# An attention step on one Trainium2 core: VectorE's addition of the projected output moves ahead of the log-sigmoid, and one normalisation moves into the next step

## The reference

```python
x = x + 0.5 * ffn(layernorm(x))        # 8 experts, the best 2 of each token
x = x + attn(layernorm(x))
x = x + 0.5 * ffn(layernorm(x))

def attn(x):                            # 16 heads of 8 features
    q, k, v = x @ Wq, x @ Wk, x @ Wv    # split into heads
    c = cumsum(log_sigmoid(x @ Wf))     # per head, along the sequence
    scores = q @ k.T * 8 ** -0.5 + c[:, None] - c[None, :]
    scores = where(causal, scores, -1e30)
    return (softmax(scores) @ v) @ Wo
```

## Time and profile before

| what | us |
|---|---|
| median of 3 runs | 460.31 |
| the three runs | 458.33, 460.38, 460.31 |
| the profiled execution | 458.89 |
| its span, first to last instruction | 456.8 |

### The profile page before, as it was taken

How to read it: one execution, slowest core, us unless ns; L and a number is a source line. 1 busy time by engine, 2 the same in 40 slices (tenths; PEclk the granted TensorE clock), 3 DMA queues, 4 the chain that set the end, 5 groups by cost and what they waited for, 6 DMA issues and landing times.

```text
span 456.8 us, 11688 instructions
## 1 busy us (share of the span) xinstructions
PE 398.6 (87%) x3280; PEld 285.1 (62%) x3296; DVE 363.6 (80%) x1284; ACT 274.9 (60%) x758; POOL 251.7 (55%) x431
## 2 busy tenths in 40 slices
PE   0778888775799999999999999999998989888884
PEld 0656666562566676667667666767776756666652
DVE  3889999987777877786797678778776459999985
ACT  4666777442266575666657566666666666667753
POOL 8977656444155536544554554455445526676654
PEclk9999999888899999999999999999999999999999
DMA  4221000025554454364355435444550000010001
GB/s 114 82 69 22 2 1 0 1 89 161 139 140 137 137 140 135 106 169 113 115 139 138 132 108 166 114 125 135 152 135 10 6 2 0 26 45 25 23 23 46
DMA packets 45024, 39.11 MB, mean 86 GB/s; under 512 B 5128, under 2 KB 41756, under 8 KB 44986
## 3 DMA queue, kind: packets, MB, share of 16 engines
q1 hardware_dynamic: 44986, 38.66, 30.2%
HBM read 22.61 MB, written 15.20 MB: 83 GB/s over the span
## 4 chain that ended last, share of the span: by engine, by line
PE 41%; POOL 24%; issue 18%; DVE 12%; DMA 2%; ACT 2%; POOLq 1%; SPq 0%; DVEq 0%; ACTq 0%
POOL m_pair L217 10%; PE bank L917 8%; PE bank L902 8%; PE bank L887 6%; POOL m_upper L221 5%; PE bank L890 4%; DVE a_neg_max L795 3%; POOL m_rstd L229 3%; PE bank L882 3%; PE bank L1009 2%; PE bank L1012 2%; DVE a_xn L815 2%; PE bank L961 1%; DMA x_all<-in_L_attn_x 1%; PE bank L1013 1%
## 5 line engine op out<-in xcount | busy, mean ns | idle before, releaser
L795 DVE TENSOR_REDUCE a_neg_max<-bank 128x2 f32<-128x512 f32 (+1 forms) x192 | 123.5, 684 | 53.6 <-PE bank L890 50.7
L684 POOL TENSOR_SCALAR_AFFINE_SELECT a_weights<-a_weights 128x512 f32<-128x512 f32 (+1 forms) x96 | 76.8, 800 | 101.9 <-ACT a_weights L738 101.7
L738 ACT ACTIVATE a_weights<-bank 128x512 f32<-128x512 f32 x192 | 104.9, 589 | 23.9 <-PE bank L902 23.4
L251 ACT ACTIVATE m_scaled<-bank,m_gates 128x128 f32<-128x128 f32 x256 | 72.3, 365 | 25.9 <-PE bank L417 25.9
L217 POOL TENSOR_TENSOR m_pair<-m_scaled 128x256 f32<-128x256 f32 x64 | 47.5, 742 | 51.0 <-ACT m_scaled L251 50.9
L902 PE MATMUL bank<-a_q_rows,a_k_rows 106*128 106x512 f32 (+1 forms) x192 | 70.8, 446 | 1.9 <-ACT a_weights L738 1.5
L294 DVE SCALAR_TENSOR_TENSOR m_lower<-bank,m_gates,m_lower 128x128 f32<-128x128 f32 x192 | 65.9, 343 | 2.3 <-issue 0.2
L887 PE MATMUL bank<-a_k_rows,a_q_rows 104*128 104x256 f32 x256 | 59.4, 335 | 0.4 <-DVE a_neg_max L795 0.4
L890 PE MATMUL bank<-a_mask,a_ident 128*128 128x256 bf16 (+1 forms) x176 | 56.3, 320 | 0.0
L917 PE MATMUL bank<-a_weights,a_v 128*32 128x128 f32 x1536 | 51.9, 276 | 0.0
L887 PEld LDWEIGHTS bank<-a_k_rows,a_q_rows 104*128 104x128 f32 x256 | 40.6, 194 | 14.5 <-DVE a_neg_max L795 9.7
(11 more groups left out here) (128 smaller groups left out, 829.1 us busy)
## 6 DMA issues: line engine op xcount, KB each, us to landing
a_k_rows<-k_stage SPq DMA_DIRECT2D x16, 416.0 KB
a_q_rows<-q_stage SPq DMA_DIRECT2D x64, 96.0 KB
k_stage<-a_k_parts SPq DMA_DIRECT2D x16, 256.0 KB, 2.2
q_stage<-a_q_parts SPq DMA_DIRECT2D x16, 256.0 KB, 2.3
a_k_heads<-k_stage SPq DMA_DIRECT2D x64, 52.0 KB
a_q_dense<-q_stage SPq DMA_DIRECT2D x16, 192.0 KB
x_all<-in_L_attn_x SPq DMA_DIRECT2D x8, 256.0 KB, 2.8
k_stage<-a_k_parts SPq DMA_DIRECT2D x16, 128.0 KB, 2.1
```

The source lines that it names most:

```text
L251: last = nc.scalar.activation(scaled[:, q % 2, j], y_high[q % 2][:, j * D:(j + 1) * D], ACT.Copy, scale=gates[:, s % 2, q, 4 + j:5 + j])
L684: nc.gpsimd.affine_select(out=diagonal, in_=diagonal, compare_op=ALU.is_ge, fill=0.0, base=0, pattern=[[0, heads.stop - heads.start], [1, P]],
L738: nc.scalar.activation(weights[n // 2][:, half:half + 4, :].rearrange("p h n -> p (h n)"), wt_bank[n % 2][:, :], ACT.Exp).then_inc(wt_exp, 1)
L795: nc.vector.tensor_reduce(neg_max[:, t, heads], score_bank[p % 2][:, :].rearrange("p (h n) -> p h n", n=(t + 1) * P), AX.X, ALU.max, negat ...
```

## The change

DVE's order within a step is changed; no instruction is added or left out, and the other engines keep their order. The addition of the projection stands directly behind the step's last row maxima, ahead of the log-sigmoid and the scan. `normalise` of a sequence's first tile moves from the end of one step into part 1 of the next, behind the row maxima 2 and 3 (so its indices go from `i - 1` to `i - 2`).

```diff
             if S:
                 row_max(i, s, 2 * j + 1)
+            if j == 1 and T:
+                normalise(i - 2, s - 2, 0)
             if s == -2 and j == 0:
...
+            if j == 5 and T:
+                dve.wait_ge(proj_ready, i - 1)
+                pair = x_all[:, bass.ds((i - 2) * 2, 2), :].rearrange("p t d -> p (t d)")
+                nc.vector.tensor_tensor(pair, pair, side_bank[:, 0:2 * D], ALU.add).then_inc(proj_added, 1)
             if j == 5 and F:
                 dve.wait_ge(log_done, n)
...
                 nc.vector.tensor_tensor_scan(neg_c[:, :], ones_row[:, :], log_sig[:, :], 0.0,
                                              ALU.mult, ALU.subtract).then_inc(c_done, 1)
-            if j == 5 and X:
-                normalise(i - 1, s - 1, 0)
-            if j == 5 and T:
-                dve.wait_ge(proj_ready, i - 1)
-                pair = x_all[:, bass.ds((i - 2) * 2, 2), :].rearrange("p t d -> p (t d)")
-                nc.vector.tensor_tensor(pair, pair, side_bank[:, 0:2 * D], ALU.add).then_inc(proj_added, 1)
```

## The result

| | before | after |
|---|---|---|
| median, us (4 runs each) | 460.35 | 453.8 |
| profiled execution, us | 458.89 | 452.93 |
| its span, us | 456.8 | 450.8 |

The account below looks back on a forecast made before the run. Bound by DVE's late row maxima at attention-step hand-overs, plus a transpose stall. Gains 2.9 + 1.84 + 0.45 less 0.2 make 5.0 us; 453.9 from the profiled run, 455.3 from the median, middle 454.6, range 452.0 to 459.0.

Parts of the forecast that it names:

- The normalisation: Moved from the step's end into DVE's idle time behind the fourth row maximum, it costs nothing; uncovered, 0.47 us a step.
- the 0.58 us: Gain per loop hand-over: the V projection into step 7 comes at 221.90 instead of 222.48.
- The five hand-overs: Between attention steps, into 4, 5, 7, 8 and 10: 0.58 us gained in each, 2.9 us together.
- The four: Hand-overs into steps 2, 11, 12 and 13: only earlier row maxima count, 0.46 us each, 1.84 us together.
- The rule: In each hand-over of the new kernel, PE's V projection comes 1.91 us behind the start of DVE's first row maximum.
- The three: Hand-overs into 3, 6 and 9: the late scan loses 0.45 us to POOL's select, leaving some 0.15 us gain each.
- Scan or select: DVE's scan starts 0.01 us ahead of POOL's causal select, so its delay is zero; the other end is 0.45 us.
- the first rival: POOL's causal select gets ahead of DVE's scan in every step: 457.6 us from the profiled run, 459.0 from the median; chance 0.24.
- Nothing collides: Scan wins in every step, all twelve hand-overs come to step 14's level: some 6.5 us gained, 452.4 us; chance 0.13.
- The late projection: Addition waits for PE's projection, delaying DVE's first row maximum 0.32 us in eleven steps: 462.4 us in all; chance 0.05.
- The tail: Last attention step: normalising the last sequence's first tile there makes PE's first expert matmul wait, 0.2 us lost.
- The sum: All hand-over gains less the loss at the end: 5.0 us together, giving 454.6 us.

Follow-up runs that it names:

- e2: Changed kernel with the addition put back behind the scan, so only the normalisation is moved: 452.98 us, 0.987 of the kernel before.
- e1: Changed kernel with the normalisation put back at the end of the step, so only the addition is moved: 459.57 us, 1.002 of the kernel before.
- e3: Changed kernel with DVE's wait for POOL's earlier split of the running sums put ahead of the log-sigmoid: 452.23 us, 0.986 of the kernel before.
- e8: Changed kernel with an unused reciprocal of 16 elements a row added between log-sigmoid and scan: 453.23 us, 0.989 of the kernel before.
- e10: Changed kernel with an unused reciprocal of 24 elements a row added between log-sigmoid and scan: 457.89 us, 0.998 of the kernel before.
- e5: Changed kernel with the addition put between log-sigmoid and scan: 452.27 us, 0.987 of the kernel before.
- e9: e5 with the last sequence's first tile normalised at the end of step 16 again, as before the change: 452.11 us, 0.987 of the kernel before.
- e0: The changed kernel run again, nothing altered, beside other follow-up kernels: 453.12 us, 0.988 of the kernel before.
- e7: Changed kernel with the projection's four matmuls on PE put behind the V products that follow them: 463.69 us, 1.011 of the kernel before.

## Why the prediction was right, step by step

**The normalisation.** Right: its new place hides it (1.29 us of idle time are left behind it), and it carries nearly the whole gain, as e2 shows. The text had split the 0.58 us into 0.46 from earlier row maxima and 0.12 from the transpose. Into step 7 the changed kernel has the first row maximum 0.40 us behind the second score matmul instead of 0.84, and the V projection 1.90 us behind that instead of 2.03, so 0.44 and 0.13. e1 gives 0.09 for the transpose alone; e2 gives 0.52 (2.87 to 2.35), of which 0.46 are the row maxima's and 0.06 the transpose's.

**The five hand-overs** into 4, 5, 7, 8 and 10: 3.01 us (2.9 forecast). **The four** into 2, 11, 12 and 13: 1.78 (1.84). **The rule** of 1.91 us from the first row maximum to the V projection: 219.21 - 217.31 = 1.90 into step 7.

**The three** into 3, 6 and 9: 0.58 us instead of 0.45, the term that was most off: the transpose alone was to give 0.15 each and gave 0.17 to 0.23. Where the collision would fall was right to the step, as was its length (a scan of 1.09 us).

**Scan or select.** The outcome was right, and so was the mechanism as far as the runs show it: in steps 2, 5 and 8 the scan comes 0.09 us later and loses, and where e3 takes these 0.09 us away it wins. The 0.01 us themselves are luck: the scan was put first by 0.01 and is, but both it and the select came 0.02 us later behind the log-sigmoid than worked out (0.46 instead of 0.44, 0.47 instead of 0.45). How thin the margin was stays open. By the recorded starts e8 wins from 0.06 us behind, which would make it 0.07 us; by the ends e8 stands no later than the changed kernel, and e10, 0.05 us later than e8, loses, which would make it less than 0.05. So the runs don't say whether 0.24 was too much for the first rival. The rival itself was sound: e10 makes it true, and by the medians 1.1 us of gain are left, where 1.3 were worked out.

L697, which runs into the log-sigmoid, takes 0.28 us instead of 0.22, held for 0.06 (0.04 forecast), and ends at 216.75 with the log-sigmoid lasting until 216.67. A hold for the whole log-sigmoid would have ended it at 216.89. The Trainium skill ("SBUF — State Buffer", section "Who interferes with whom") has the first to issue keep the shared ports for its whole instruction. That one is held and the other runs free is what all 226 meetings show; a hold up to the winner's recorded end is not. Taken as the held one's start and the time that it took too long, the hold ends 0.14 us ahead of that end where the log-sigmoid holds L697 (216.53 of 216.67) and where L849 holds the select (0.27 of 0.41 us), 0.15 ahead where the select holds the scan (154.73 of 154.88), and 0.19 where the scan holds the select (217.19 of 217.38). Whether the winner is done with its reading by then, the rows don't say. That such a hold would have given the sum of the first rival doesn't follow from the text's own times: L697 would have ended at 218.95 + 0.40 + 0.22 = 219.57, and what the scan, due at 219.39, met first would have been the rest of L697, 0.18 us, not the select.

**The other rivals.** Nothing collides: e3, e5 and e9 make it true, 1.4 to 1.5 us below e0 in the stretch, 452.1 to 452.3 us (452.4 worked out). The late projection: e7, 463.69 us (462.4 worked out); DVE stood idle for 0.95 us ahead of the addition, where the text had put the addition 0.78 us behind its slot.

**The tail**: 0.20 us, as forecast, and for the reason given. **The sum**: 5.32 in the stretch, where 5.19 were forecast (2.9 + 1.84 + 0.45), and 0.20 lost in the tail. The span is 6.0 us shorter; the remaining 0.9 is, as far as the runs show, not the change's: 0.59 ahead of step 2, which varies as said, and 0.33 ahead of step 15, where PE idles for 0 to 0.56 us from run to run for no reason that the profile names. By the medians the change is worth 6.55 us here and 5.49 in e0 (453.12 against the 458.61 of the kernel before, on the same chip), against 5.0 forecast. That 454.6 lies so near 453.8 is in part luck of the starting point, which the text put between a quick run and the median; from the median it would have been 455.3.

## What to carry to other kernels

A wait at the head of an engine's list is worth only what the next wait leaves of it: taking away the 3.3 us of the transpose alone gained nothing (e1), because the row maxima were due at nearly the same time; a stretch in the same trace where the suspected work is missing (step 14) priced it rightly. Where instructions of two engines hold each other up, the order of two starts a few hundredths of a microsecond apart can be worth 0.5 us a step; look for meetings near that edge, and put other work, or a wait, where it moves the start to the safe side (e3, e5).

## What was not expected of the hardware

- Between the causal select on POOL and a DVE instruction with two SBUF operands one is held and the other runs free in all 226 meetings, and the held one gets through 0.14 to 0.19 us ahead of the other's recorded end (four meetings, worked out above).
- Behind a short reciprocal the scan was recorded with 0.62 us instead of 0.68 and ended no later (e8); the 0.24 us of the reciprocal were free.
- A register operation for a wait, between two DVE instructions of which the second needs the first one's result, cost 0.09 us; ahead of both it was free (e3).
- At the loop's jump back DVE's sequencer takes 0.28 to 0.30 us from its branch to its next operation in e1, and DVE idled 0.21 to 0.23 us where no longer instruction covered it.
- The reciprocal costs by the element: 0.24 us for 16 a row, 0.29 for 24, 0.94 for 128, some 6 ns each.
